# Cross-attention on one core: z and k transposed by DMA after a GpSimd split, q's second half stacked from GpSimd's queue, and another opening

## What is computed

```python
x = (hidden - mu) * rsqrt(var + LN_EPS) * ln_gamma + ln_beta
Q = split_heads(x @ Wq.T);  K = split_heads(ctx);  V = split_heads(ctx)
scores = einsum('bhsd,bhtd->bhst', Q, K) * HEAD_DIM ** -0.5
scores = where(mask, scores, -inf)
attn = einsum('bhst,bhtd->bhsd', softmax(scores), V)
out = hidden + merge_heads(attn) @ Wout.T
```

## Time and profile before

| | |
|---|---|
| median of 3 runs | 630.49 us (628.89 to 630.75) |
| the profiled execution | 630.62 us |
| its span | 628.8 us |
| mean granted clock of TensorE | 0.975 |
| instructions | 12852 |
| moved by DMA | 68.62 MB, mean 109 GB/s |

### The profile page before, as it was taken

How to read it: one execution, slowest core, us unless ns; L and a number is a source line. 1 busy time by engine, 2 the same in 40 slices (tenths; PEclk the granted TensorE clock), 3 DMA queues, 4 the chain that set the end, 5 groups by cost and what they waited for, 6 DMA issues and landing times.

```text
span 628.8 us, 12852 instructions
## 1 busy us (share of the span) xinstructions
PE 589.5 (94%) x4769; PEld 396.2 (63%) x4769; DVE 385.0 (61%) x841; ACT 430.8 (69%) x1321; POOL 112.8 (18%) x131
## 2 busy tenths in 40 slices
PE   4878879999999999999999999999999999998897
PEld 4667657655776567655776567755776567644443
DVE  5575977478654885388654886288645882278211
ACT  3342978778766886678766886678666885699740
POOL 2320440035000530044000520044001520000000
PEclk9889689999999999999999999999999999999899
DMA  9774321443344252343344152333344132321202
GB/s 282 267 223 128 114 73 55 122 126 99 106 117 130 60 163 56 107 117 105 100 125 130 52 170 57 99 119 109 96 124 134 63 89 57 98 51 67 71 1 101
DMA packets 37344, 68.62 MB, mean 109 GB/s; under 512 B 9009, under 2 KB 11041, under 8 KB 37282
## 3 DMA queue, kind: packets, MB, share of 16 engines
q1 hardware_dynamic: 36994, 67.60, 35.9%
q10 hardware_dynamic: 288, 0.20, 0.1%
HBM read 33.56 MB, written 8.39 MB: 67 GB/s over the span
## 4 chain that ended last, share of the span: by engine, by line
PE 71%; DVE 14%; ACT 8%; issue 3%; DMA 2%; ACTq 1%; SPq 1%; DVEq 0%
PE mm L453 24%; PE mm L478 17%; PE pv L537 10%; PE score L525 9%; PE score L499 6%; DVE nmax L826 6%; ACT score L653 6%; PE pv L415 2%; PE pv L428 2%; DMA ctx_sb<-in_ctx 1%; ACT probs L670 1%; DVE o_buf L868 1%; PE pv L382 1%; DVE wqT L748 1%; DVE t_f L777 1%
## 5 line engine op out<-in xcount | busy, mean ns | idle before, releaser
L653 ACT ACTIVATE score<-score,nmax 128x256 f32<-128x256 f32 x512 | 230.1, 465 | 47.7 <-DVE nmax L826 47.6
L453 PE MATMUL mm<-zT,wqT 128*128 128x256 f16 x1536 | 186.6, 276 | 0.0
L826 DVE TENSOR_REDUCE nmax<-score 128x2 f32<-128x512 f32 x256 | 163.8, 684 | 37.0 <-PE score L499 36.9
L478 PE MATMUL mm<-woT,aT 128*128 128x512 f16 x768 | 183.6, 379 | 1.5 <-DVE o_buf L868 1.5
L670 ACT ACTIVATE probs<-score 128x1024 f32<-128x1024 f32 x128 | 123.9, 1022 | 73.4 <-PE score L525 73.1
L453 PEld LDWEIGHTS mm<-zT,wqT 128*128 128x128 f16 x1536 | 151.5, 99 | 23.0 <-issue 2.9
L478 PEld LDWEIGHTS mm<-woT,aT 128*128 128x128 f16 x768 | 74.7, 97 | 73.2 <-DVE o_buf L868 4.4
L653 ACT ACTIVATION_READ_ACCUMULATOR score<-score,nmax 128x1 f32 x512 | 114.7, 224 | 0.0
L861 DVE TENSOR_TENSOR aT<-pv,aT 128x256 f16<-128x256 f32 x64 | 26.9, 423 | 114.7 <-ACT aT L676 113.9
L499 PE MATMUL score<-k_stack,q_stack 97*128 97x256 f16 x512 | 79.6, 279 | 10.5 <-ACT score L653 9.4
L499 PEld LDWEIGHTS score<-k_stack,q_stack 97*128 97x128 f16 x512 | 47.9, 99 | 46.4 <-ACT score L653 22.9
(11 more groups left out here) (62 smaller groups left out, 352.2 us busy)
## 6 DMA issues: line engine op xcount, KB each, us to landing
k_stack<-kT SPq DMA_DIRECT2D x192, 64.0 KB, 2.0
q_stack<-qT SPq DMA_DIRECT2D x180, 64.0 KB, 2.0
x_nat<-in_x SPq DMA_DIRECT2D x8, 1024.0 KB, 5.4
ctx_sb<-in_ctx SPq DMA_DIRECT2D x8, 1024.0 KB, 6.3
res<-in_x SPq DMA_DIRECT2D x32, 256.0 KB, 2.9
out<-o_buf SPq DMA_DIRECT2D x32, 256.0 KB, 2.0
probs<-in_L_xattn_Wq SPq DMA_DIRECT2D x8, 512.0 KB, 7.8
probs<-in_L_xattn_Wout SPq DMA_DIRECT2D x8, 512.0 KB, 4.5
```

The lines of the kernel that those rows point to most:

```text
L453: last = pe.matmul(mm[i % 2][:, m2 * S:(m2 + 1) * S], wqT[:, wp, k, m * P:(m + 1) * P], zT[:, zp, k, :], start=(v2 == 0), stop=(v2 == KT * ...
L478: last = pe.matmul(mm[i % 2][:], aT[:, ap, k, st * P:(st + 1) * P], woT[:, wp, k, nh * 512:(nh + 1) * 512], start=(v == 0), stop=(v == O_M ...
L653: last = act.activation(score[n % 2][:, j, :], score[n % 2][:, j, :], ACT.Exp, bias=nmax[:, st, h, j, gl:gl + 1], accum_out=sums[:, st, h, ...
L826: dve.tensor_reduce(nmax[:, st, h, at, gl], score[n % 2][:, at, :], AX.X, ALU.max, negate=True).then_inc(max_done, 1)
```

## The change

- **z.** VectorE now applies mean and gamma, then the reciprocal deviation and beta, in natural layout (`centre`, `normalise`: one pass over 128x1024 each per row block, gamma and beta broadcast to all partitions by DMA). GpSimd splits the result into `z_nat`, a buffer of its own, and SyncE transposes it into `zT` by four transposing transfers of 128x1024 float16 per batch (`turn_z`). TensorE's z transposes and VectorE's `z_scale` are gone, except for batch 0, where TensorE still transposes z and ScalarE and VectorE split it.
- **k.** GpSimd builds, in natural layout, for 16 heads of one block of context rows a tile of 128 columns per head: k high twice, k low, and 32 extra columns with the mask and the units of the log-sum rows (`k_split`: a cast, a copy, a subtraction). Four such slots are used, in batch 2 and later in the memory of `probs`, for batch 0 in k_stack's other buffer, for batch 1 in `aT`, `res` and `o_buf`. SyncE turns each by one transposing transfer of 128x2048 float16 straight into `k_stack` (`turn_k`). TensorE's k transposes, `k_scale`, `kT` and the 24 stacking and 2 mask transfers per batch are gone. ScalarE's first writes to `probs` wait for the slots to be read.
- **q.** The 12 transfers that stack q's second half are issued by GpSimd instead of SyncE, after it has split z and before it splits k.
- **Scales.** q and k are no longer scaled by 2 and 0.5.
- **The opening.** x of batch 0 comes in two transfers. Only 12 fills of Wq and two of q's four stand before batch 0's scores; the other four fills of Wq, two of q and all 16 fills of Wout lie in batch 0's steps (`WQ_STEPS`, `Q0_AT`, `WO_STEPS`). SyncE and GpSimd share the stacking of batch 0's q.

The diff, cut to its core:

```diff
+        def k_nat(a, c):
+            if known(a, 0):
+                flat = k_stack[:, 1].rearrange("p h g j s -> p (h g j s)")[:, c * HEADS * P:(c + 1) * HEADS * P]
+            elif known(a, 1) and c < 2:
+                flat = aT[:, c].rearrange("p g s -> p (g s)")
+            elif known(a, 1):
+                flat = f16((res, o_buf)[c % 2][:].rearrange("p a d -> p (a d)"))
+            else:
+                flat = f16(probs[:, c // 2, c % 2].rearrange("p j s -> p (j s)"))
+            return flat.rearrange("p (n d) -> p n d", n=HEADS)
...
-        Z_STEPS, K_STEPS = (0, 1, 2, 3), (6, 7, 8, 9)
-        WO_FIRST = W_FILLS // 2
-        WO_STEPS = (4, 5, 10, 11, 12, 13, 14, 15)
+        WQ_EARLY = 12
+        WO_STEPS = {n: (n - 4,) for n in range(4, 12)} | {n: (2 * n - 16, 2 * n - 15) for n in range(12, 16)}
+        Q0_SPLITS = {2: 2, 5: 3}
+        WQ_STEPS = {0: (12,), 1: (13,), 2: (14, 15)}
...
+            def turn_z(a):
+                for st in range(ST):
+                    sp.wait_ge(z_lo, (a - 1) * ST + st + 1)
+                    if st == 0:
+                        sp.wait_ge(q_ready, a * FILLS)
+                    for part in range(2):
+                        sp.dma_start_transpose(zT[:, part, :, st * P:(st + 1) * P], z_nat[:, st, part]).then_inc(z_in, DMA)
+            def turn_k(a, pa, c):
+                sp.wait_ge(k_done, 2 * (4 * a + c + 1))
...
+                sp.dma_start_transpose(k_turned(pa, c), k_nat(a, c).rearrange("p n d -> p (n d)")).then_inc(k_in[c // 2], DMA)
...
+                    if not last:
+                        sp.wait_ge(pv_ready, b * G)
+                        load_c(b + 1, 1 - pb)
+                        turn_z(b + 1)
+                    if more:
+                        load_x(b + 2)
+                    store_out(b - 1, 0)
+                    load_res(b - 1, 2)
+                    if not last:
+                        turn_k(b + 1, 1 - pb, 0)
+                        turn_k(b + 1, 1 - pb, 1)
+                    store_out(b - 1, 1)
+                    load_res(b - 1, 3)
+                    if not last:
+                        turn_k(b + 1, 1 - pb, 2)
+                        turn_k(b + 1, 1 - pb, 3)
+                    store_out(b - 1, 2)
                 fill_l_rows(b, 0)
                 fill_l_rows(b, 1)
...
+            def z_split(a, st):
+                pool.wait_ge(norm_done, a * ST + st + 1)
+                if a > 1 and st == 0:
+                    pool.wait_ge(z_in, (a - 1) * 2 * ST * DMA)
+                pool.tensor_copy(z_nat[:, st, 0], x_nat[:, st]).then_inc(z_hi, 1)
+                pool.wait_ge(z_hi, (a - 1) * ST + st + 1)
+                pool.tensor_tensor(z_nat[:, st, 1], x_nat[:, st], z_nat[:, st, 0], ALU.subtract).then_inc(z_lo, 1)
...
+                pool.tensor_copy(to[:, :, 0:2 * DH].rearrange("p n (r d) -> p n r d", r=2), of.unsqueeze(2).to_broadcast([P, HEADS, 2, DH])).then_inc(k_hi, 1)
+                pool.tensor_copy(to[:, :, 3 * DH:3 * DH + K_EXTRA], k_extra[:, a, tt].unsqueeze(1).to_broadcast([P, HEADS, K_EXTRA])).then_inc(k_done, 1)
+                pool.wait_ge(k_hi, 4 * a + c + 1)
+                pool.tensor_tensor(to[:, :, 2 * DH:3 * DH], of, to[:, :, 0:DH], ALU.subtract).then_inc(k_done, 1)
...
+            for c in range(4):
+                k_split(0, 0, c)
+            fill_q0_tile(0, (2, 3))
+            fill_q0_tile(2, range(J))
+            for st in range(ST):
+                z_split(1, st)
+            fill_q0_tile(3, range(J))
+            for c in range(4):
+                k_split(1, 1, c)
+            for a in range(2, B):
+                for st in range(ST):
+                    z_split(a, st)
+                fill_q_stack(a - 1)
+                for c in range(4):
+                    k_split(a, a % 2, c)
+            fill_q_stack(B - 1)
...
                     elif u == 0:
-                        pe.wait_ge(split_done, z_fill(a, 3) + 1)
+                        pe.wait_ge(z_in, a * 2 * ST * DMA)
...
+                if first and n == 0:
+                    act.wait_ge(wo_ready, W_FILLS)
+                elif n in (0, 2) and not last:
+                    act.wait_ge(k_in[n // 2], 2 * (b + 2) * DMA)
                 act.activation(probs[:, g % 2, tt], score[n % 2][:], ACT.Exp).then_inc(exp_done, 1)
...
+            def centre(a, st):
+                dve.wait_ge(rstd_step, (a + 1) * RSTD_STEPS)
...
+                dve.scalar_tensor_tensor(out=x_nat[:, st], in0=x_nat[:, st], scalar=mean_var[:, st, 0:1], in1=gamma_b[:],
+                                         op0=ALU.subtract, op1=ALU.mult).then_inc(centre_done, 1)
             def normalise(a, st):
-                dve.wait_ge(rstd_step, (a + 1) * RSTD_STEPS)
-                dve.tensor_scalar(x_nat[:, st], x_nat[:, st], mean_var[:, st, 0:1], rstd[:, st:st + 1],
-                                  ALU.subtract, ALU.mult).then_inc(norm_done, 1)
+                dve.wait_ge(centre_done, a * ST + st + 1)
+                dve.scalar_tensor_tensor(out=x_nat[:, st], in0=x_nat[:, st], scalar=rstd[:, st:st + 1], in1=beta_b[:],
+                                         op0=ALU.mult, op1=ALU.add).then_inc(norm_done, 1)
```

524 lines of the change are left out of this document (222 added, 302 removed).

## The result

| | before | after |
|---|---|---|
| median | 630.49 us (627.75 to 631.21) | 624.61 us (624.01 to 626.08) |
| ratio | | 0.9928, 95% interval 0.9901 to 0.9955 |
| profiled execution, span | 630.62, 628.8 us | 625.53, 623.7 us |
| granted clock, mean | 0.975 | 0.964 |

The change makes the kernel 0.7% faster. The interval leaves no change out, but the forecast was 611 us: of the 19.5 us it promised, 5.9 came.

A forecast was written before the change was run, and what follows sets the result against it. TensorE was taken to set a middle batch. 630.6 - 21.1 (transposes removed) + 6.6 (VectorE and GpSimd waits) - 5 (start) = 611 us; the forecast's own range was 603 to 619, the whole range 597 to 633.

The forecast's parts named there:

- its floor of 34.5: Middle batches' first half: must stay above the last batch's 34.5 us, where ScalarE limits a step; 36.2 us expected.
- first rival: Whole kernel: everything fits, no engine holds up the other, the start has no hole; 597.5 us, chance 0.15.
- third rival: Before step 8: GpSimd's queue dearer than the two measured, TensorE waits for q's second half; 643 us, chance 0.15.
- +6.6 us over six: Step 10 of middle batches: VectorE's log-sum operations and GpSimd's k work hold each other up, 1.1 us a batch.
- second rival: Step 10: VectorE and GpSimd exclude each other in full, some 3.2 us a batch reach TensorE; 624 us, chance 0.13.
- high end of four subtractions (4.6): Step 10: VectorE's four log-sum operations each wait for a whole GpSimd subtraction, 4 x 1.16 = 4.6 us a batch.
- fourth rival: SyncE: transposing transfers hold the queue, log-sum rows late from 4.9 us each; near 625 at 5.5, chance 0.06.
- -5 us: Start: first score near 37 us, 23 us earlier, but work moves into batch 0's first half; ends -12 and +8.
- 46 us or more: Batch 0's first half: VectorE's 34.18 us grow to some 42, so the half lasts at least 46 us.
- The wait on GpSimd's stack at step 12: Batch 0: q's fourth fill stacked by GpSimd at 80.6 us, while step 12 needs it near 74.

The follow-up runs named there:

- dummy transposes: Changed kernel with eight times four unused TensorE transposes of the identity put back in each of the six middle batches: 643.52 us.
- k over step 10: Changed kernel with GpSimd starting on k only at step 8 in the middle batches, so its run covers VectorE's log-sum operations: 634.39 us.
- old opening: Changed kernel with all 16 Wq, four q and 8 Wout fills again before batch 0, VectorE's passes over batch 1's x ahead of batch 0's steps: 624.41 us.
- GpSimd's part alone: Changed kernel with GpSimd preparing pieces 1 to 3 of batch 1's k after VectorE's first log-sum, load order unchanged: 618.32 us.
- late k: Changed kernel with pieces 1 to 3 of batch 1's k prepared after VectorE's first log-sum, and the last two Wout tiles issued ahead of k transposes: 618.00 us.
- both repairs: Changed kernel with late k, and Wout fills split in the step that transposes them in steps 12 to 15 alone: 608.95 us.
- the run that moved them: Kernel with both repairs, and batch 0's last q fill a step later (two halves, steps 4 and 5 instead of 3 and 4): 607.15 us.

## Why the prediction was right and wrong

**The middle batches: right, and the size too.** Taken off TensorE were 3.52 us a batch by the step lengths of the earlier trace rows; four of six batches show 3.43 or 3.44 (70.28 less 66.84), and the dummy transposes give them back to within 0.05 us. The half ends at 36.36, not at its floor of 34.5. Batches of 66.8 us were the first rival's sign, not the forecast's 67.9. Two batches lose 1.2 and 0.5 us, on GpSimd's stack and on the log-sum rows' transfer; in the other kernels other batches lose such amounts, or none. The last batch was forecast unchanged and is 1.6 us shorter, by the higher granted clock in its second half; that is luck of the execution.

**GpSimd's queue: the third rival was out, and the value taken was too high.** It was 0.49 us per transfer, where the text took 0.9 between 0.65 and 1.3. The lower bound was wrong as a bound: nothing in the rows said that GpSimd's queue couldn't be cheaper than SyncE's. The stack's transfers took 8.0 us to land in the median, not 2.0, and it was still in time for step 8 in five of six middle batches. In batch 2 the last took 11.0, and step 8 came 0.69 us late: the wait of the third rival, by way of the landing that the text had put at 2.0 us, not of the issue.

**The wait between VectorE and GpSimd: in the wrong place.** The term "+6.6 us over six" rested on k pieces that cover steps 7 to 12. With transfers of 0.49 us, and pieces of 2.65 instead of 3.0 us, the run ends 4.3 us before the log-sum operations of step 10: the middle batches paid nothing. Where the run does cover it, the price is 1.75 us a batch (k over step 10), between the 1.1 taken and the second rival's 3.2. The one place where cover and operations met in the changed kernel is batch 0, which the text didn't look at for it: there one operation paid 6.58 us, more than the high end of four subtractions (4.6) that the text set for all four operations together. The Trainium skill, page "SBUF — State Buffer", section "SBUF: two separate sides", has the pair of ports as a lock held for a whole instruction. The endings in the k-over-step-10 run agree with it; the 6.58 us in batch 0 span the starts of seven of GpSimd's instructions, which that rule alone doesn't give.

**Transposing transfers: held the queue, and used up the margin in the middle.** The text took a landing of 4.5 us and a short issue; k's took 5.1 and the four of batch 2 held the queue for 14.2 us, 3.5 each, under the 4.9 where the fourth rival begins. But the text let k's start 14.4 us into the batch and gave z's no time on the queue. They held it for 15.8 us, so that k's first went out at 18.1 and the log-sum rows at 34.5 us into a half of 36.4. In four batches that was in time, in two it made TensorE wait 0.40 and 0.38 us. For the opening see the old opening.

**The start: the step that failed.** "I take **-5 us**; ends -12 and +8" was measured as +15.3, outside both ends. The first score was right (36.2 for 37), and so was the shift of work into the first half. The half was said to last "46 us or more", from VectorE's busy time, and GpSimd's list was given some 7 us more. It lasted 80.7 us although VectorE was busy for only 50 of them and GpSimd for 29. What the text didn't follow was the order inside a step. First, the hold-up at step 11: 5.7 us of start and 6.3 us of time (624.61 to 618.32) by the kernel with GpSimd's part alone. Second, the loop between two Wout fills' splits, the next maxima and the 16 q matmuls: 8.4 us of start (135.82 to 127.45, late k without and with the repair of the loop) and 9.0 us of time, 7.9 of them in steps 12 to 15 and part of it by the lower granted clock that comes with TensorE's idle time. What is left of the way from 143.5 to 127.5, 2.0 us, came with the order of loads, but is no more than the same opening varies by; as a cause it isn't shown. The wait on GpSimd's stack at step 12 that the text named didn't come: with 0.49 us per transfer the last one was issued by 69.3 us, and step 12 came at 82.7. With both repairs the start is 127.5, 0.8 us under the start before. The forecast's -5 is still 4 us away; TensorE's waits of 1.63 and 3.03 us for Wq splits are of that size, but the run that moved them didn't remove them.

**The sum.** 628.8 + 15.3 - 18.8 - 1.6 = 623.7. No rival had this: the second (624) and the fourth (near 625 at 5.5 us) came to the right number, but by a loss of 2.4 us or more in each middle batch that the middle batches don't show. That is luck.

## What to carry to other kernels

Work woven into steps must be followed by the order in which each engine's queue holds it, not by busy sums: a split placed behind the next step's maxima made a loop through three engines that cost 8 us in four steps, and idle TensorE time was paid twice, as waiting and as a lower granted clock. The same placement was right where a step had one fill and wrong where it had two, so such a rule is tried for each kind of step apart. Short VectorE operations with two SBUF inputs should be kept out of the time in which GpSimd runs without a gap; moving GpSimd's run behind them cost nothing here.

## What the runs showed of the hardware

One VectorE operation of 32 elements per partition took 6.58 us, and 5.58 to 6.53 in five other kernels, where it began inside an uninterrupted run of GpSimd's instructions in batch 0, and each time it ended within 0.1 us of the end of that run; beside a similar run in the middle batches the like operations took at most 1.2 us each. Twelve transfers of 64 KB issue from GpSimd in 5.88 us (0.49 each), cheaper than SyncE's 0.67. They land after 2.0 us, as SyncE's do, in the last batch, and after 8.0 us in the median where transposing transfers are under way. A transposing transfer of 256 KB holds its issuing queue for 1.2 to 1.5 us in the kernel without GpSimd's q transfers from batch 1 on, and for 1.2 to 6.1 us in the one with them, about 4 in batch 2; one of 512 KB holds it for 1.8 to 7.0 us. With them the DMA engines' share of a first half is 0.98 at 204 GB/s, where 0.41 went with 128 GB/s. Their packets are small: 101984 of the execution's 122522 are under 512 B, where it was 9009 of 37344 before the change. The granted clock of the same 290 matmuls in the last half was 0.95 in some executions and 1.00 in others, which is worth 1.4 to 1.6 us.
